# Expert steps of two units, new fill tables, and pair 1's front inside pair 0's first block

## The chip, the cores and the metric

The kernel runs on one core of a Trainium2 chip. A core has five engines that run side by side: TensorE (PE; its weight loads are listed as PEld), VectorE (DVE), ScalarE (ACT), GpSimd (POOL) and SyncE (SP), which here only starts DMAs. Each engine works through its own instructions in program order, and they wait for one another on semaphores. The metric is the device time of one execution in microseconds; lower is better.

## The reference, cut to what matters

```python
h = tok_ref(x, ...)                       # 16 images -> 49 patch tokens + cls, width 192 (convolutions, wavelets)
h = concatenate([h, txt], axis=1)         # + 128 text tokens -> 178 tokens an image
h = h + attn_ref(layernorm(h), ...)       # 12 heads of 16, diagonal masked except token 0, softmax, projection
h = h + ffn_ref(layernorm(h), ...)        # what follows:
    logits = gamma * zscore(Q @ K.T * scale)     # z-score of each row, then softmax, 12 heads
    x = layernorm(src + attn @ Wo.T + bo)
    gate_scores = softmax(x @ Wg.T + bg)         # 4 experts, the best 2 of each token are kept
    h = relu(x @ W1[e] + b1[e]); y = h @ W2[e] + b2[e]   # 192 -> 768 -> 192, all 4 experts
    ff = sum(y * combine); out = layernorm(x + ff)
```

All data is float32. Queries and keys are cut into three bfloat16 parts; the first expert matrix and its input are cut into a high and a low part.

## The kernel before, in words

**Stages.** The token stage (convolutions) takes the first part of the program. Then the 16 images are treated as 8 *pairs*. A pair goes through three blocks: block 0 is the first attention (`s = 0`), block 1 the second one (`s = 1`), and the third is the experts (MoE). They are pipelined over *rounds*: a round runs block 0 of pair `a`, block 1 of pair `b = a - 1`, the front of block 0 (turn-in, query, key, value) of pair `nxt = a + 1`, and the experts of pair `m = a - 2`. Engines run `pe_round`, `act_round`, `dve_round`, `sp_round` and `pool_round`, each with this same order, called by `rounds` (L1496). Round 0 has only `a = 0, nxt = 1`; round 1 has `a = 1, b = 0, nxt = 2`; rounds 2 to 6 are complete; round 7 has `a = 7, b = 6, m = 5`; round 8 has `b = 7, m = 6`; the last has `m = 7` alone.

**An attention block.** The input is normalised on DVE (`xn`), turned by PE (`pe_turn_in`), copied by ACT, projected to query and key (`pe_query`, `pe_key`), evacuated by ACT, split by DVE (`dve_split`), stored to DRAM and loaded back stacked (`stack` on SP). A *max pass* computes all logits once so that DVE can take the row maxima (`pe_max_pass`, `dve_max_pass`, 6 steps of two heads); the maxima are turned, copied and put as three more rows under the queries by DMA (`stack_max`); an *exp pass* computes the logits again with the maximum in them, ACT exponentiates, and PE multiplies by the values (`pe_values`). `pe_out` and `dve_out` normalise, project and add. Block 1 also has a *deviation* part (`pe_deviation`, `act_deviation`) that ends in the factor of the z-score, with which DVE scales the query before its split (`query` in `dve_front1`). After block 1 of pair `b`, DVE makes `x2`, PE turns it (L964), ACT and DVE make `x2T_hi` and `x2T_lo`, and PE computes the gate (L977).

**The experts as filling.** The experts of a pair are 24 *units* of 128 hidden channels. A unit has a *first* part F(u), five matmuls over 370 columns (L644) into PSUM bank `4 + u % 2`, the ReLU on ACT (L679) into `hid[u % 2]`, and a *second* part S(u), three float32 products of 192 columns, shown as six matmuls (L666). After every sixth unit DVE adds the expert's result to `acc` (L694, `expert`), which waits for that unit's second part. The class `Moe` cuts this into half steps: 0 is F(0), 1 is nothing, 2 is F(1), 3 is S(0), 4 is F(2), 5 is S(1), and so on to 48 (turning `comb`, S(23)) and 49 (`bias`, L654). At each named point of a round, `moe.point(name)` issues the number of half steps that the table says (`FILL`, in round 7 `FILL_A7`, in round 8 `FILL_B7`), on PE, ACT and DVE alike; `moe.rest()` issues what is left, in `pe_round` after the next pair's key and ahead of the turning of `x2`. The key places in `pe_round` are: "start"; turn-in of block 1; "norm"; query; "query"; key; "key"; value; the deviation part with "kc", "g", "u"; "ss"; max pass 0; ("split", 0); ("rows", 0); exp pass 0; max pass 1; ("split", 1); out of block 0 with ("turn", 0), ("back", 0); ("rows", 1); exp pass 1; out of block 1 with ("turn", 1), ("back", 1); the next turn-in; "next norm"; query; "next query"; key; rest. `("rows", 1)` stands under `if a is not None`, so that round 8 skips it.

**The beginning.** Before round 0 pair 0's front is computed, then `act_weights` and `dve_weights` cut the expert weights, which lie in four raw pieces of 1536 columns in `probs`, `qst1` and `kst1`; `dve_weights` ends with setting part of `kst1` to one (L1426), since that buffer held raw weights until then. Round 0 runs block 0 of pair 0 and then the front of pair 1, whose text is loaded into `h0` only once pair 0's residual has been added (`res_ready`).

## Time and profile before

| | |
|---|---|
| median of 3 runs | 1287.3 us (1286.83 to 1294.15) |
| the profiled execution | 1291.78 us, its span 1290.0 us |
| PE busy | 1095.4 us, 85% |
| DVE, ACT busy | 682.1 us, 399.7 us |
| mean granted TensorE clock | 0.884 |

By the stages of the profile: the token stage and pair 0's front last until 199.4 us, round 0 until 268.0, round 1 until 396.6, rounds 2 to 6 take 119.5 to 119.9 us each and end at 994.9, round 7 ends at 1117.2, round 8 at 1227.4, and the last round's experts run until 1279.0. The boundaries are the first turn-in of a round, or its gate's end.

How to read it: a busy time of PE is modelled from the start of each matmul, and the records of two neighbours overlap, so the distance from start to start is the better length. Idle time is shown in brackets with what ended it; "issue" means that no semaphore in the profile explains it.

### The profile page before, as it was taken

Reading aid. Unit: us, or ns where it says so; the run is one execution under the profiler, and the core shown is the slowest. Engines: PE = TensorE matmul, PEld = TensorE weight load, DVE = VectorE, ACT = ScalarE, POOL = GpSimd, SP = SyncE. Lnnn points to the kernel's source line nnn. Section 1 sums busy time; section 2 is a strip of 40 time slices with the busy share of each in tenths; the row PEclk is TensorE's granted clock in tenths of the full one; section 3 lists DMA queues with packets and bytes.
Section 4 is the critical chain, followed back from the end, with each engine's and each line's share of the span. In section 5 each row is a group of like instructions: output and inputs, shape, how many; then the busy total and the mean of one; then the engine's idle time right before and its main releaser. Section 6 shows DMA issues by size and latency. Waiting matters only on the chain.

```text
span 1290.0 us, 18666 instructions
## 1 busy us (share of the span) xinstructions
PE 1095.4 (85%) x7404; PEld 802.2 (62%) x7404; DVE 682.1 (53%) x1874; ACT 399.7 (31%) x905; POOL 54.1 (4%) x89
## 2 busy tenths in 40 slices
PE   7898645587779999999999999999999999985896
PEld 4343323354448668857776786678578667773795
DVE  1467685345454466654763674655557652632332
ACT  1222221212232433334323434333343234221321
POOL 6011100000000000000000000000000000000000
PEclk9898855755779989989998999899999989895988
DMA  8000051053005202320422043014204220022000
GB/s 296 0 1 0 16 152 26 7 97 61 11 7 119 49 8 56 78 43 9 84 51 44 8 105 66 13 34 100 44 8 82 51 43 2 1 64 29 1 10 8
DMA packets 38478, 60.74 MB, mean 47 GB/s; under 512 B 5060, under 2 KB 30264, under 8 KB 38072
## 3 DMA queue, kind: packets, MB, share of 16 engines
q1 hardware_dynamic: 36112, 56.84, 20.5%
q10 hardware_dynamic: 2280, 2.72, 0.7%
q8 instruction: 58, 0.95, 0.3%
q14 instruction: 28, 0.23, 0.1%
HBM read 42.76 MB, written 16.34 MB: 46 GB/s over the span
## 4 chain that ended last, share of the span: by engine, by line
PE 63%; DVE 13%; ACT 4%; issue 3%; DMA 3%; SPq 1%; POOL 0%; DVEq 0%; ACTq 0%; POOLq 0%
PE PS L666 14%; PE PS L644 11%; PE PS L755 7%; DVE mx L1271 6%; PE PS L849 5%; PE PS L763 5%; PE PS L790 5%; PE PS L796 3%; PE PS L805 2%; PE PS L858 2%; DMA qst<-mrows 1%; PE PS L887 1%; PE PS L977 1%; ACT probs L1031 1%; SPq L1471 1%
## 5 line engine op out<-in xcount | busy, mean ns | idle before, releaser
L666 PE MATMUL PS<-w,hid 128*128 128x192 f32 x1152 | 232.1, 339 | 3.0 <-DVE acc L694 1.8
L679 ACT ACTIVATE hid<-PS,b 128x370 f32<-128x370 f32 x192 | 109.1, 569 | 331.6 <-PE PS L644 329.8
L666 PEld LDWEIGHTS PS<-w,hid 128*128 128x128 f32 x1152 | 199.0, 197 | 12.8 <-issue 4.7
L1271 DVE TENSOR_REDUCE mx<-PS 128x2 f32<-128x356 f32 x288 | 129.8, 522 | 131.6 <-PE PS L790 103.5
L1031 ACT ACTIVATE probs<-PS 128x356 f32<-128x356 f32 x288 | 112.9, 484 | 35.6 <-PE PS L790 20.6
L790 PE MATMUL PS<-kst,qst 96*128 96x178 bf16 x384 | 71.5, 284 | 31.7 <-DMA kst<-scr_k 13.6
L644 PE MATMUL PS<-x2T_hi,w_hi 128*128 128x370 f32 x192 | 91.7, 478 | 0.0
L755 PE MATMUL PS<-xT,w_at 96*96 96x370 f32 x192 | 76.0, 546 | 8.9 <-ACT q L998 5.2
L805 PE MATMUL PS<-masks,ident_bf 128*128 128x256 bf16 (+1 forms) x288 | 79.9, 278 | 0.0
L790 PE MATMUL PS<-qst,kst 99*128 99x178 bf16 x384 | 58.0, 254 | 21.7 <-DMA qst<-mrows 17.5
L849 PE MATMUL PS<-probs,va 128*17 128x178 f32 x1536 | 70.8, 327 | 6.4 <-ACT probs L1031 6.4
L790 PEld LDWEIGHTS PS<-kst,qst 96*128 96x128 bf16 x384 | 27.2, 106 | 66.0 <-DVE mx L1271 30.7
L1292 DVE RECIPROCAL rs<-PS 128x36 f32<-128x36 f32 x16 | 6.1, 383 | 114.4 <-PE PS L858 114.4
L644 PE MATMUL PS<-x2T_hi,w_lo 128*128 128x370 f32 x192 | 66.2, 345 | 0.0
L644 PE MATMUL PS<-x2T_lo,w_hi 128*128 128x370 f32 x192 | 66.1, 344 | 0.0
L644 PE MATMUL PS<-x2T_hi,w_rest 128*128 128x370 f32 x192 | 66.1, 344 | 0.0
L644 PE MATMUL PS<-x2T_lo,w_rest 128*128 128x370 f32 x192 | 65.6, 342 | 0.0
L755 PEld LDWEIGHTS PS<-xT,w_at 96*96 96x96 f32 x192 | 33.4, 182 | 41.9 <-ACT q L998 8.9
L790 PEld LDWEIGHTS PS<-qst,kst 99*128 99x128 bf16 x384 | 28.7, 101 | 46.9 <-issue 30.8
L849 PEld LDWEIGHTS PS<-probs,va 128*17 128x17 f32 x1536 | 41.0, 99 | 24.4 <-ACT probs L1031 9.3
L694 DVE SCALAR_TENSOR_TENSOR acc<-PS,comb,acc 128x192 f32<-128x192 f32 x72 | 25.5, 410 | 54.3 <-PE PS L666 54.2
L377 DVE SCALAR_TENSOR_TENSOR dwo<-pad_l,chan,dwo 96x441 f32<-96x441 f32 x48 | 38.0, 793 | 27.9 <-ACT cw L301 26.4
(222 smaller groups left out, 1724.4 us busy)
## 6 DMA issues: line engine op xcount, KB each, us to landing
qst<-scr_q SPq DMA_DIRECT2D x96, 144.0 KB, 4.8
scr_q<-qs SPq DMA_DIRECT2D x16, 432.0 KB, 3.3
scr_k<-ks SPq DMA_DIRECT2D x16, 432.0 KB, 4.7
kst<-scr_k SPq DMA_DIRECT2D x16, 432.0 KB, 5.0
kst<-scr_k SPq DMA_DIRECT2D x16, 288.0 KB, 5.9
cols<-in_x_cols SPq DMA_DIRECT2D x6, 392.0 KB, 8.2
w<-in_w SPq DMA_DIRECT2D x1, 2304.0 KB, 25.2
kst<-scr_k SPq DMA_DIRECT2D x16, 144.0 KB, 6.3
```

What stands on the lines that cost most here:

```text
L377: ch.link(nc.vector.scalar_tensor_tensor(out=out, in0=image_rows(PAD_OF[r][:, 0, :], tap_offset(t), n), scalar=col(C_DW + 18 * r + t), in1 ...
L644: ins = nc.tensor.matmul(PS[:, 4 + u % 2, 0:XN], w[:, f], x[:, plane, 0:XN], start=(k == 0), stop=(k == 4))
L666: ins = nc.tensor.matmul(tile_psum((6, 7), i), hid[u % 2][:, 128 * i:128 * i + 128], w2[:, u, :], start=(j == 0 and i != 1), stop=(j == FT ...
L679: nc.scalar.activation(hid[u % 2][:, 0:XN], PS[:, 4 + u % 2, 0:XN], ACT.Relu, bias=b1[:, u:u + 1]).then_inc(S["h_ready"], 1)
L755: ins = nc.tensor.matmul(PS[0:HC, FRONT[s][m], 0:XN], w_at[:, w, k, HC * m:HC * m + HC], x[:, k, 0:XN], start=(k == 0), stop=(k == 1))
L763: ins = nc.tensor.matmul(tile_psum(banks, i), tile_cols(x, k, i), w_at[:, w, k, :], start=(k == 0), stop=(k == 1))
L790: ins = nc.tensor.matmul(PS[:, bank, T * b:T * b + T], still[0:rows_, h, TP * b:TP * b + NTXT], move[0:rows_, h, TP * b:TP * b + T], start ...
L796: ins = nc.tensor.matmul(PS[64 * b:64 * b + 64, 2, T * g:T * g + T], still[0:rows_, 2 * u + g, TP * b + NTXT:TP * b + TP], move[0:rows_, 2 ...
L805: ins = nc.tensor.matmul(own, ident_bf[:], m.rearrange("p (b j) -> p b j", b=2), start=False, stop=True, skip_group_check=True)
L849: ins = nc.tensor.matmul(PS[32 * q:32 * q + VW, 3, T * b:T * b + T], va[s][:, 2 * i + b, h, :], pr, start=(i == 0), stop=(i == 1), skip_gr ...
L1031: nc.scalar.activation(probs[:, u % PROB_UNITS, bank, :], PS[:, bank, 0:T2], ACT.Exp)\
L1271: nc.vector.tensor_reduce(out, PS[:, g, 0:T2].rearrange("p (b j) -> p b j", b=2), AX.X, ALU.max)\
```

## The change

It has four parts.

1. **Half steps of two units.** `MOE_STEPS` goes from 50 to 26. Step (d, even) is F(2d) and F(2d+1), step (d, odd) is S(2d) and S(2d+1). All fill tables are rewritten for it. Step (12, even) only turns `comb`. DVE's expert sums follow the odd steps of d = 2, 5, 8 and 11. `("rows", 1)` is now issued in every round.
2. **The bias behind the turning.** `pe_round` issues all steps but the last, turns `x2`, and only then issues the bias step. DVE's and ACT's order stays: all steps, then `x2T`.
3. **Pair 1's front inside pair 0's block.** Round 0 is replaced by `pe_first`, `act_first`, `dve_first` and `sp_first`. Pair 1's input lies in `h1_fin` instead of `h0`, its text is loaded at the start (semaphore `txt_early`), and its front uses PSUM banks 4 and 5.
4. **Raw weights in other pieces.** 1536, 1536, 2304 and 768 columns, in `probs` and `qst1` only, so that `kst1` is free and is set to one at the start of the token stage; the chain in `dve_weights` is one shorter.

```diff
-MOE_STEPS = 2 * UNITS + 2
+DUOS = UNITS // 2
+MOE_STEPS = 2 * DUOS + 2
 FILL = {
-    "start": 4, "norm": 1, "query": 4, "key": 3, "value": 0, "kc": 2, "g": 2, "u": 1, "ss": 2,
-    ("max", 0): (0, 0, 0, 0, 0, 0), ("split", 0): 2, ("rows", 0): 4, ("exp", 0): (0, 0, 0, 0, 0, 0), ("out", 0): 0,
-    ("max", 1): (0, 0, 0, 0, 0, 0), ("split", 1): 2, ("turn", 0): 2, ("back", 0): 1, ("rows", 1): 1,
-    ("exp", 1): (1, 0, 1, 1, 0, 2), ("out", 1): 0, ("turn", 1): 2, ("back", 1): 1, "next turn": 0, "next norm": 3,
-    "next query": 2,
+    "start": 2, "norm": 1, "query": 2, "key": 2, "value": 0, "kc": 1, "g": 1, "u": 1, "ss": 1,
+    ("max", 0): (0, 0, 0, 0, 0, 0), ("split", 0): 1, ("rows", 0): 2, ("exp", 0): (0, 0, 0, 0, 0, 0), ("out", 0): 0,
+    ("max", 1): (0, 0, 0, 0, 0, 0), ("split", 1): 1, ("turn", 0): 1, ("back", 0): 1, ("rows", 1): 0,
+    ("exp", 1): (0, 1, 0, 1, 0, 1), ("out", 1): 0, ("turn", 1): 1, ("back", 1): 0, "next turn": 0, "next norm": 2,
+    "next query": 1,
 }
 FILL_A7 = {
-    "start": 4, "norm": 4, "query": 4, "key": 0, "value": 0, "kc": 1, "g": 2, "u": 1, "ss": 2,
-    ("max", 0): (0, 1, 0, 0, 0, 0), ("split", 0): 2, ("rows", 0): 4, ("exp", 0): (1, 0, 0, 0, 0, 0), ("out", 0): 0,
-    ("max", 1): (0, 0, 1, 0, 0, 0), ("split", 1): 2, ("turn", 0): 2, ("back", 0): 1, ("rows", 1): 0,
-    ("exp", 1): (1, 2, 0, 0, 0, 1), ("out", 1): 1, ("turn", 1): 2, ("back", 1): 0, "next turn": 0, "next norm": 4,
+    "start": 2, "norm": 2, "query": 2, "key": 0, "value": 0, "kc": 1, "g": 1, "u": 0, "ss": 1,
+    ("max", 0): (0, 0, 0, 0, 0, 0), ("split", 0): 1, ("rows", 0): 2, ("exp", 0): (0, 0, 0, 0, 0, 0), ("out", 0): 0,
+    ("max", 1): (0, 0, 0, 0, 0, 0), ("split", 1): 1, ("turn", 0): 1, ("back", 0): 1, ("rows", 1): 0,
+    ("exp", 1): (0, 1, 0, 0, 0, 1), ("out", 1): 0, ("turn", 1): 1, ("back", 1): 0, "next turn": 0, "next norm": 0,
...
 FILL_B7 = {
-    "start": 4, "norm": 1, "query": 3, "key": 4, "value": 0, "kc": 2, "g": 0, "u": 2, "ss": 14,
-    ("max", 0): (0, 0, 0, 1, 1, 0), ("split", 0): 0, ("rows", 0): 0, ("exp", 0): (0, 0, 0, 0, 0, 0), ("out", 0): 1,
-    ("max", 1): (0, 0, 0, 0, 0, 0), ("split", 1): 1, ("turn", 0): 1, ("back", 0): 2, ("rows", 1): 4,
-    ("exp", 1): (1, 2, 0, 0, 0, 2), ("out", 1): 1, ("turn", 1): 2, ("back", 1): 0, "next turn": 0, "next norm": 3,
+    "start": 0, "norm": 0, "query": 2, "key": 1, "value": 0, "kc": 0, "g": 0, "u": 0, "ss": 10,
+    ("max", 0): (0, 0, 0, 0, 0, 0), ("split", 0): 0, ("rows", 0): 0, ("exp", 0): (0, 0, 0, 0, 0, 0), ("out", 0): 0,
+    ("max", 1): (0, 0, 0, 0, 0, 0), ("split", 1): 1, ("turn", 0): 0, ("back", 0): 0, ("rows", 1): 3,
+    ("exp", 1): (0, 1, 0, 0, 0, 1), ("out", 1): 0, ("turn", 1): 1, ("back", 1): 0, "next turn": 0, "next norm": 0,
...
@@ the token stage's DVE block
-                    nc.vector.memset(kst[0][SROWS:128, :, :], 1.0)
                     for s in range(2):
+                        nc.vector.memset(kst[s][SROWS:128, :, :], 1.0)
@@ buffers
+        W1_PARTS = ((0, 0, 1536, flat_probs[:, 0:1536]), (0, 1536, 3072, flat_probs[:, 1536:3072]),
+                    (1, 0, 2304, flat_qst[:, 0:2304]), (1, 2304, 3072, flat_probs[:, 3072:3840]))
+        def front(s, r):
+            return (2, 3) if s else (4, 5) if isinstance(r, int) and r == 1 else (0, 1)
+        def h_in(r):
+            return h1_fin if isinstance(r, int) and r == 1 else h0
@@ class MoePe
+            def step(self, d, odd):
                 pe, m = self.eng, self.m
+                if odd and d == DUOS:
                     self.bias()
                 elif odd:
+                    for u in range(2 * d, 2 * d + 2):
+                        self.second(u)
+                elif d == DUOS:
                     pe.wait_ge(S["comb_ready"], at(m, 1, 1))
...
+                else:
+                    for u in range(2 * d, 2 * d + 2):
+                        self.first(u)
@@ class MoeDve
+                elif odd and (2 * d + 2) % FT == 0:
+                    self.expert((2 * d + 2) // FT - 1)
@@ pe_round, and the like for ("rows", 1) in act_round and dve_round
             if a is not None:
                 pe_out(pe, 0, a, moe)
-                moe.point(("rows", 1))
+            moe.point(("rows", 1))
+            if a is not None:
                 pe.wait_ge(S["pr_read", 0], at(a, 1, 1))
...
-            moe.rest()
+            moe.steps(MOE_STEPS - 1 - moe.done)
             if b is not None:
                 pe.wait_ge(S["x2_ready"], at(b, 1, 1))
...
                 ins.then_inc(S["x2T_psum"], 1)
+            moe.rest()
@@ in place of round 0
+        def pe_first(pe):
+            pe_turn_in(pe, 0, 0)
+            pe_query(pe, 0, 0)
+            pe_key(pe, 0, 0)
+            pe_value(pe, 0, 0)
+            pe_turn_in(pe, 0, 1)
+            pe_query(pe, 0, 1)
+            none = NoMoe()
+            pe.wait_ge(S["v_ready", 0], 1)
+            pe_max_pass(pe, 0, 0, none)
+            pe_max_rows(pe, 0, 0)
+            pe_key(pe, 0, 1)
+            pe_exp_pass(pe, 0, 0, none)
+            pe.wait_ge(S["e_done", 0], 3 * HH)
+            pe_out(pe, 0, 0, none)
+            pe.wait_ge(S["pr_read", 0], 1)
+            pe_value(pe, 0, 1)
+        def act_first(act):
+            act_turn_in(act, 0, 0)
+            act_query(act, 0, 0)
+            act_key(act, 0, 0, None)
+            act_weights(act)
+            act_turn_in(act, 0, 1)
+            act.wait_ge(S["q_split", 0], 1)
+            act_query(act, 0, 1)
+            act.wait_ge(S["w_split"], 1)
+            act_max_rows(act, 0, 0)
+            act.wait_ge(S["k_split", 0], 1)
+            act_key(act, 0, 1, None)
+            none = NoMoe()
+            act_exp_pass(act, 0, 0, none)
+            act_out(act, 0, 0, none)
+        def dve_first(dve):
+            none = NoMoe()
+            tok_norm(dve, 0, 1)
+            splits = dve_front0(dve, 0)
+            tok_norm(dve, 1, PAIRS)
+            splits(None)
+            dve_value(dve, 0, 0)
+            splits = dve_front0(dve, 1)
+            dve_weights(dve)
+            dve_max_pass(dve, 0, 0, none)
+            dve.wait_ge(S["q_stored", 0], 16)
+            dve.wait_ge(S["k_stored", 0], 16)
+            splits(None)
+            dve_out(dve, 0, 0, none)
+            dve_norm1(dve, 0)()
+            dve_value(dve, 0, 1)
+        def sp_first(sp):
+            stack(sp, 0, 0, "q")
+            stack(sp, 0, 0, "k")
+            stack_max(sp, 0, 0)
+            stack_store(sp, 0, 1, "q")
+            stack_store(sp, 0, 1, "k")
+            sp.wait_ge(S["pv_psum", 0], 3)
+            stack_load(sp, 0, 1, "q")
+            stack_load(sp, 0, 1, "k")
-            one_round(eng, 0, None, 1, None, FILL)
@@ gpsimd
                 nc.gpsimd.memset(h0[:, 2, :], 0.0)
+                nc.gpsimd.memset(h1_fin[:, 2, :], 0.0)
...
                 pool.wait_ge(S["tok_ready"], 2)
+                image(pool, 1)
                 rounds(pool, pool_round)
```

## Rows read from the trace of the kernel before

**Rows 1.** The page's parts 1 and 2: engines, and TensorE's granted clock in 40 slices.
```profile
PE 1095.4 (85%) x7404; PEld 802.2 (62%) x7404; DVE 682.1 (53%) x1874; ACT 399.7 (31%) x905; POOL 54.1 (4%) x89
...
PEclk9898855755779989989998999899999989895988
```

**Rows 2.** Busy by stage: window, its length, busy of PE, PEld, DVE, ACT, POOL; clock.
```profile
199.40:249.50 50.10, 29.03 (x259) 17.85 (x260) 21.80 (x71) 10.43 (x27) 1.35 (x3) 0.67 0.02 5
...
516.50:636.30 119.80, 113.43 (x878) 87.50 (x876) 71.47 (x212) 44.45 (x105) 2.52 (x4) 0.97 0.25 50
...
1117.20:1227.40 110.20, 84.94 (x569) 68.85 (x566) 41.85 (x114) 30.24 (x66) 1.33 (x2) 0.84 0.14 28
```

**Rows 3.** Timeline of DVE, pair 0's front to round 0: start, us, what.
```profile
162.46 0.88 DVE L1123 BATCH_NORM_STATS2 stat<-h 128x6 f32<-128x192 f32 x3 [1.10 <-POOL h L1402]
...
166.02 0.96 DVE L1135 TENSOR_SCALAR xn<-h,mv,lsc 128x192 f32<-128x192 f32 x3
...
186.38 0.71 DVE L1156 TENSOR_TENSOR va<-PS,rows 50x192 f32<-50x192 f32 x2
...
196.07 3.90 DVE L1426 MEMSET kst<- 32x4608 bf16 x1 [1.02 <-issue]
...
244.62 0.17 DVE L151 SCALAR_TENSOR_TENSOR lsc<-lsc 128x3 f32<-128x3 f32 x1
```

**Rows 4.** Timeline of PE in the same stretch, to round 1's first turn-in.
```profile
199.42 0.46 PE L790 MATMUL PS<-kst,qst 96*128 96x178 bf16 x2 [13.56 <-DMA kst<-scr_k]
...
212.25 0.80 PE L823 MATMUL PS<-ident,mpart 128*36 128x128 f32 x3 [2.71 <-DVE mpart L1280]
...
217.54 0.46 PE L790 MATMUL PS<-qst,kst 99*128 99x178 bf16 x2 [4.50 <-DMA qst<-mrows]
...
251.85 5.00 PE L755 MATMUL PS<-xT,w_at 96*96 96x370 f32 x8 [0.88 <-ACT xT L991]
...
268.01 1.49 PE L747 MATMUL PS<-ident,xn 128*96 128x128 f32 x6
```

**Rows 5.** The page's part 5: a unit's first matmul and its second one.
```profile
L644 PE MATMUL PS<-x2T_hi,w_hi 128*128 128x370 f32 x192 | 91.7, 478 | 0.0
...
L644 PE MATMUL PS<-x2T_hi,w_lo 128*128 128x370 f32 x192 | 66.2, 345 | 0.0
```

**Rows 6.** Timeline of PE in the last round: two units in a row.
```profile
1236.17 0.47 PE L644 MATMUL PS<-x2T_hi,w_hi 128*128 128x370 f32 x1
...
1237.15 1.14 PE L666 MATMUL PS<-w,hid 128*128 128x192 f32 x6
1237.99 0.47 PE L644 MATMUL PS<-x2T_hi,w_hi 128*128 128x370 f32 x1
```

**Rows 7.** Who PE waited for in round 7: total us, times, longest.
```profile
PE PS L763 <- ACT oT L1048: 0.9, 1, 0.9
PE PS L790 <- DVE h L1304: 0.9, 1, 0.9
```

**Rows 8.** Timeline of PE at the end of round 2: next turn-in, gate.
```profile
491.56 0.82 PE L747 MATMUL PS<-ident,xn 128*96 128x128 f32 x6
...
512.34 0.24 PE L977 MATMUL PS<-gate_a,x2T_hi 128*128 128x8 f32 x1
```

**Rows 9.** Timeline of DVE there: splits, last expert sum, x2T_lo.
```profile
500.77 0.52 DVE L1142 CAST qs<-q 96x712 bf16<-96x712 f32 x1
...
507.13 1.07 DVE L694 SCALAR_TENSOR_TENSOR acc<-PS,comb,acc 128x192 f32<-128x192 f32 x3 [0.42 <-PE PS L666]
...
511.23 0.96 DVE L1389 TENSOR_TENSOR x2T_lo<-PS,x2T_hi 128x768 fp32r<-128x768 f32 x1 [0.81 <-ACT x2T_hi L1114]
```

**Rows 10.** Timeline of DVE in round 8, before block 1's max pass.
```profile
1152.74 1.07 DVE L694 SCALAR_TENSOR_TENSOR acc<-PS,comb,acc 128x192 f32<-128x192 f32 x3 [12.64 <-PE PS L666]
1153.84 0.96 DVE L1257 SCALAR_TENSOR_TENSOR q<-q,chan,rem 96x712 f32<-96x712 f32 x1
```

**Rows 11.** Timeline of PE there: what its max pass waited.
```profile
1170.02 0.75 PE L790 MATMUL PS<-kst,qst 96*128 96x178 bf16 x4 [13.03 <-issue]
```

**Rows 12.** Who PE waited for in the last round.
```profile
PE PS L666 <- DVE acc L694: 1.4, 3, 0.5
PE PS L654 <- DVE acc L694: 1.2, 1, 1.2
```

More of the change, by code:

```diff
@@ L111 @@
+    ("exp", 1): (0, 1, 0, 0, 0, 1), ("out", 1): 0, ("turn", 1): 1, ("back", 1): 0, "next turn": 0, "next norm": 0,
+    "next query": 0,
 }
@@ L670, in build, with step @@
         class MoeAct(Moe):
-            def step(self, u, odd):
+            def step(self, d, odd):
                 act, m = self.eng, self.m
-                if not odd and u < UNITS:
+                if odd:
+                    return
+                if d == DUOS:
+                    act.wait_ge(S["ct_psum"], at(m, 1, 1))
+                    nc.scalar.copy(combT[:, 0:XN], PS[0:E, 4, 0:XN]).then_inc(S["ct_ready"], 1)
+                    return
+                for u in range(2 * d, 2 * d + 2):
                     act.wait_ge(S["h_psum"], at(m, UNITS, u + 1))
@@ L727, in build, with steps @@
         class NoMoe:
+            done = 0
             def rest(self):
+                pass
+            def steps(self, n):
                 pass
@@ L995, in act_query @@
             for h in range(2):
[L996 removed]
+                for src, c in zip(by_token(front(s, r)[h]), (slice(0, NTXT), slice(NTXT, T))):
                     if s == 0:
@@ L1009, in act_key @@
             for h in range(2):
-                for src, c in zip(by_token(FRONT[s][h]), (slice(0, NTXT), slice(NTXT, T))):
+                for src, c in zip(by_token(front(s, r)[h]), (slice(0, NTXT), slice(NTXT, T))):
                     if s == 0:
@@ L1406, in act_weights @@
         def act_weights(act):
-            act.wait_ge(S["raw_in"], 16 * 2 * WCH)
-            for n in range(2 * WCH):
-                nc.scalar.copy(w1_part(n), raw[n]).then_inc(S["w_cast"], 1)
+            act.wait_ge(S["raw_in"], 16 * len(W1_PARTS))
+            for rest, lo, hi, raw in W1_PARTS:
+                nc.scalar.copy((w1_rest if rest else w1_hi)[:, lo:hi], raw).then_inc(S["w_cast"], 1)
         def dve_weights(dve):
```

137 lines of the change are left out of this document (58 added, 79 removed).

## The prediction, made before the changed kernel was run

> **What bounds the kernel now.** I read the page first: PE is busy for 85% of the span, twice as long as ACT and more, and its granted clock falls from 0.9 to 0.5 and 0.7 in the slices of rounds 0 and 1, again near the end [rows 1]. The busy times by stage then show three regimes [rows 2]. Round 0 has no expert work: PE is busy 29.0 of 50.1 us, at a clock of 0.67, and latencies between engines set its length. In a complete round PE is busy 113.4 of 119.8 us at 0.97; there are five of these, so there the time is PE's own work plus the few places where no filling covers a wait. Round 8 has 84.9 of 110.2 us busy at 0.84. So a change of order pays where PE has nothing to do (rounds 0, 1, 8), and in rounds 2 to 6 it can only move waits, each counted five times.
>
> **Pair 1's front.** Before, round 1 starts at 268.01, after pair 1's turn-in, query, key and value. In the new order it needs only `xn` of block 1. Step by step. DVE finishes pair 0's value at 187.1, and then does pair 1's normalisation, which took 162.46 to 166.98 for pair 0, 4.5 us; it lost the 3.9 us memset behind the weights, so the weights end at 199.97 + 4.5 - 3.9 - 1.0 (the gap ahead of the memset) = 199.6 [rows 3]. The memset itself is moved to the head of the token stage, where DVE then waits for loads; I price it at 0, and at 3.9 us if that wait were not there. PE gets `xn` at 191.7, needs 1.5 for the turn, 0.9 for ACT's copy and 5.0 for the query at the low clock, and is done at 199.1; the max pass began at 199.42 on the DMA of the keys and still does [rows 4]. The four extra text DMAs are issued on SP before it waits for the query split, 1.3 us of an idle queue: 0. POOL's extra memset and two copies are also in idle time: 0. Behind the turn of the maxima (ends 213.05) PE now does pair 1's key, 5.0 us as the query at the low clock, to 218.1, where the exp pass began at 217.54 [rows 4]; ACT evacuates that key (1.3 us) ahead of its first exponential, 219.5 in place of 218.25. Cost 1.3 us; the bounds are 0 (high clock) and 3. Pair 0's residual sum's root ends at 244.79 [rows 3], now 246.1; `xn` takes 0.96 (the row at 166.02), so round 1's turn-in starts at 247.1. Pair 1's value, 4 us of PE, ends before that. Gain 268.0 - 247.1 = **20.9 us**. What is late next is the same chain as before, block 0's end into block 1's front; the splits of pair 1 lie in the exp pass, where DVE is idle.
>
> **The order of two units.** A unit takes 1237.99 - 1236.17 = 1.82 us from start to start [rows 6]: F is 0.85 and S 0.97. The first matmul of a unit is shown as 478 ns, the others as 345 [rows 5], and in the new order every other F follows an F instead of an S. A plain reading gives 96 times 133 ns = 12.8 us of gain. I take 0: the 12 instructions of 192 columns and 370 columns, read from start to start, fill the 1.82 us if each S instruction takes 0.162 us and each F one 0.17, and the six S then reach 0.14 us into the record of the next F. The Trainium skill ("TensorE: Matmul & The Clock Gate", Part 1) states that the distance of back-to-back matmuls is set by their columns and the clock, with about 2.5 ns on top; by that rule the sum stays as it is. The means of the records, taken at their word, remain a rival below. S(2d) must wait for the ReLU of F(2d), 0.57 us under F(2d+1), 0.85 us: 0.
>
> **Rounds 2 to 6.** The same 24 F and 24 S are issued, so only covers change; I went slot by slot with F = 0.85 and S = 0.97. ("rows", 1) goes from one F to nothing, and PE waits for DVE to read the projection; ("back", 1) goes from one F to nothing, and PE waits for ACT's copy. Both already stand so in `FILL_A7`, where the waits are 0.9 us each [rows 7]: +0.85 each. "norm" and "u" had an F against latencies of about 1.05 and 1.15 and get two units' worth: -0.2 and -0.3. Split 0 gets 0.1 more: -0.1. Exp pass 1 gets one S more in its idle spots: -0.4 (0 to -1.0). The end of the round is the largest. Before, from turn-in to gate it is 512.34 - 491.56 = 20.8 us with 4 F and 6 S in it [rows 8]; the new table has 2 F and 4 S there, so 17.15 us if nothing waits. But the last expert sum now comes ahead of DVE's two splits instead of behind them [rows 9], and PE has only the turning of `comb`, of `x2`, the bias and the value after the key. DVE: S(23) ends 8.7 us after the turn-in, sum until 10.5, query split until 13.5, key split until 16.5 (500.77 to 506.7 is 6.0 us for both), bias 0.95, `x2T_lo` 0.96: the gate starts at 18.5, +1.4 (bounds +0.3 and +4.6, the whole F and S that followed the key). The 1.16 us wait ahead of the bias, which disappears by the new place of the bias, is inside that figure. DVE's second expert sum now comes ahead of block 1's query split, 1.1 us later into a DMA that landed about 1.5 us early: +0.1 (0 to 1.1). Sum per round: 1.7 - 0.6 - 0.4 + 1.4 + 0.1 = +2.2, five times **+11**, bounds 0 and +27.
>
> **Round 7.** "u" has no step any more, +0.9; three steps that stood inside passes go to the rest, +1.3 by half their length; the end has the bias wait covered, -0.9: **+1.3**, bounds -1 and +4.
>
> **Round 8.** This is where the new table looks best and does least. PE waited 13.0 us for block 1's stacked query [rows 11], and the query was late because DVE stood 12.64 us in the expert sum that "ss" contains, with the query scaling right behind it [rows 10]. The new "ss" has 10 double steps, and its second sum needs S(11), that is 8 F and 10 S after the deviation product, 16.5 us, where it was 5 F and 5 S and a wait of 1.1, 10.2 us: +6.3. The front before it has 4 F and 2 S instead of 8 F and 7 S, 8.2 us less work, of which waits of 3 to 6 us appear: -2 to -5, and PE is at its low clock for part of it. So the max pass starts 1 to 4 us later, though PE idles there again. The newly reached ("rows", 1) fills the 4.4 us wait for the maxima but can run over it by 3 at the low clock, exp pass 1 is shorter by as much, and the end wins 2.4 with less rest work ahead of `x2`'s turning and no bias wait. Together **-1**, bounds -5 and +4.
>
> **Last round.** Waits for the sums of 1.4 us are covered by a second F: -1.2; the bias wait of 1.2 loses what the turning of `comb` covers: -0.3 [rows 12]. **-1.5**.
>
> **Sum.** -20.9 + 11 + 1.3 - 1 - 1.5 = -11 us. Against the profiled execution's 1291.8 us this is 1280.8; the median of the runs is 4.5 us lower, 1287.3, and -11 makes **1276 us**, 0.9% less. About 1%, 12.9 us, is what a measurement here tells from no change, so 1274.4 and 1300.2 are the borders.
>
> **Rivals.** (1) *Moved covers cost nothing.* Small waits of 0.9 us could be taken back where another engine catches up; for it: PE never waits over 1.2 us in a complete round. Against it: the same two slots do show 0.9 in round 7. Rounds 2 to 6 at 0 give -22, 1265. (2) *The longer record is real*: -11 - 12.8 = -24, 1263. Against it: the sum of starts above. (3) *Half the overlap*: ACT has pair 1's key and query ahead of the exponentials and DVE pair 1's norm ahead of the weights; if PE's and DVE's 5 us each fall on the chain, 10 of the 20.9 us go, 1286. For it: both are within 0.3 us of the DMA that hides them. (4) *Slower than before, by the end of the round*: after the last key nothing covers DVE's chain expert sum, two splits, bias, `x2T_lo`. Should the sum start late, the gate comes 4.6 us later instead of 1.4, and rounds 2 to 6 cost 27: with the rest, +5, 1292. It decides from 2.2 us more a round on; only with round 8 at its bad bound as well would it pass 1300. (5) *The change doesn't do what it says* holds for round 8 alone, and is in the sum.
>
> **Chances.** The forecast 0.53, ±6 about 1276, of which a third lies below 1274.4; rival 1 0.17, rival 2 0.06, rival 3 0.12, rival 4 0.12. Faster by over 1%: 0.18 + 0.17 + 0.06 and a little = 0.42. Slower by over 1%: 0.08, from the end of rival 4. Within 1%: 0.50. The range takes in rivals 1 and 3 and most of 4: 1263 to 1291.
>
> **What would show it.** Round 1's first turn-in at 247, not 268 us. Complete rounds of about 122 us in place of 119.8, with new waits of 0.8 us at L763 and L790, a wait of 2 us or more ahead of L977, and none ahead of L654. The means of L644's first matmul lower, but a unit pair still 3.64 us from start to start. In round 8 DVE's longest wait for L666 near 16 us and PE's wait for the max pass above 13. The forecast is wrong if complete rounds stay at 119.8 or grow by over 4 us, or if the exp pass of pair 0 starts after 221.

## The result, and the profile after

| | before | changed |
|---|---|---|
| median of 17 runs each, on one chip | 1289.79 us (1283.86 to 1297.93) | 1300.54 us (1288.67 to 1313.86) |
| ratio to before | | **1.0066, 95% [1.0043, 1.0090]** |
| the profiled execution | 1291.78 us | 1313.86 us, span 1312.1 us |
| mean granted TensorE clock | 0.884 | 0.868 |

The changed kernel is a little slower, within 1%. The forecast was 1276.0 us, within 1% too, but on the other side, and 1300.5 lies outside its range. The profiled execution of the changed kernel is the longest and slowest of its 17 runs, so its stages overstate the usual loss; experiment 6, profiled at 1295.12 us with the same code up to round 7, is set beside it below.

The page, parts 1 and 2, answers to [rows 1]:

```profile
PE 1126.7 (86%) x7404; PEld 831.0 (63%) x7404; DVE 680.4 (52%) x1874; ACT 399.1 (30%) x905; POOL 56.3 (4%) x90
...
PEclk9898867656789898989898999799988999886998
```

PE has the same 7404 instructions and is busy 31.3 us longer. DVE and ACT are not. Its mean granted clock is lower (0.868, before 0.884), and single records below are longer where the clock is low (a gate product 0.35 us, before 0.24); the second half of the last row has eight digits under 9 where it had seven. The busy times by stage, columns as in [rows 2]: pair 0's block (the max pass to round 1's turn-in), one complete round, round 8.

```profile
201.00:248.70 47.70, 37.82 (x286) 22.99 (x284) 25.83 (x64) 12.30 (x35) 0.66 (x1) 0.79 0.35 65
...
634.60:760.90 126.30, 116.66 (x877) 91.83 (x876) 71.78 (x211) 44.42 (x105) 2.48 (x4) 0.93 0.24 47
1133.90:1252.50 118.60, 94.10 (x584) 75.18 (x585) 44.26 (x127) 31.59 (x69) 1.42 (x2) 0.82 0.13 26
```

**Pair 1's front** took the path that was forecast. PE's timeline, against [rows 4]:

```profile
197.11 1.51 PE L762 MATMUL PS<-ident,xn 128*96 128x128 f32 x6 [6.49 <-DVE xn L1193]
...
204.94 0.31 PE L805 MATMUL PS<-kst,qst 96*128 96x178 bf16 x2 [0.52 <-DMA kst<-scr_k]
...
221.00 0.33 PE L805 MATMUL PS<-qst,kst 99*128 99x178 bf16 x2
...
222.98 0.33 PE L805 MATMUL PS<-qst,kst 99*128 99x178 bf16 x2 [0.85 <-ACT probs L1070]
...
248.67 1.52 PE L762 MATMUL PS<-ident,xn 128*96 128x128 f32 x6 [1.14 <-DVE xn L1193]
```

Pair 1's turn and query stand in what was one 13.56 us wait for the keys' DMA; 6.49 us of it are left ahead of the turn and 0.52 ahead of the max pass. The exp pass starts at 221.00, right behind pair 1's key, so nothing is left of the 4.50 us wait for the maxima; the 0.85 us stand one step later, for ACT's exponentials. In this execution the whole beginning is 5.3 us late (pair 0's turn-in at 172.39, 167.1 before). Round 1 starts at 248.67 in place of 268.01; counted from pair 0's turn-in that is 76.3 us in place of 100.9, a gain of 24.6 where the forecast has 20.9. Part of the rest is clock: behind pair 1's turn and query the max pass runs at the high level, and DVE's row maxima, which follow it, take 7.93 us in place of 9.97.

**By stages**, measured from gate to gate (the gate is the product on `gate_a`, L977 before, L994 after):

| | before | after | difference | forecast |
|---|---|---|---|---|
| to round 1's gate | 390.9 | 373.3 | -17.6 | -20.9 |
| rounds 2 to 6 | 599.8 | 635.3 | **+35.5** | +11 |
| round 7 | 119.4 | 122.8 | +3.4 | +1.3 |
| round 8 | 114.8 | 119.3 | +4.5 | -1 |
| gate of round 8 to the end | 65.0 | 61.4 | -3.7 | -1.5 |

The sum is +22.1, the difference of the two spans (1312.1 - 1290.0). The five complete rounds take 122.9, 129.3, 126.3, 129.8 and 127.0 us. Experiment 6, with the same code in the first three rows, has -22.4, +28.7 and +3.4 there.

**The end of a complete round.** PE's timeline, against [rows 8]; L661 is the bias, L994 the gate, L673 the second parts of the first two units, and the last row the next round's turn-in:

```profile
747.12 1.21 PE L661 MATMUL PS<-b,hid 4*128 4x192 f32 x6 [0.82 <-ACT hid L686]
...
751.89 0.35 PE L994 MATMUL PS<-gate_a,x2T_hi 128*128 128x8 f32 x1 [1.15 <-DVE x2T_lo L1450]
...
757.67 3.42 PE L673 MATMUL PS<-w,hid 128*128 128x192 f32 x12
760.92 0.82 PE L762 MATMUL PS<-ident,xn 128*96 128x128 f32 x6
```

From the next pair's turn-in (733.85) to the gate it is 18.0 us; 18.5 was forecast. But from the gate to block 1's turn-in it is 9.0 us, where two first and two second parts at 0.85 and 0.97 and the gate's 1.3 make 5.0. One gate instruction is 0.35 us long, 0.24 in [rows 8]; twelve matmuls of the second parts are 3.42 us, 2.18 elsewhere. Windows of 10 us about this place, after (first three) and before (last three), columns as above; the middle one of each begins 2 us ahead of the gate:

```profile
739.90:749.90 10.00, 9.18 (x48) 6.92 (x48) 9.62 (x19) 3.98 (x10) 0.00 (x0) 1.00 0.17 44
749.90:759.90 10.00, 8.85 (x33) 8.38 (x32) 5.47 (x21) 1.35 (x3) 0.00 (x0) 0.51 0.82 133
759.90:769.90 10.00, 10.00 (x54) 8.64 (x54) 6.60 (x27) 4.06 (x9) 0.00 (x0) 0.98 0.45 90
```
```profile
859.20:869.20 10.00, 8.84 (x51) 7.39 (x50) 8.26 (x16) 2.77 (x7) 0.00 (x0) 1.00 0.39 86
869.20:879.20 10.00, 9.88 (x58) 8.28 (x58) 6.82 (x25) 3.46 (x6) 0.00 (x0) 1.00 0.86 148
879.20:889.20 10.00, 10.00 (x54) 8.57 (x53) 8.54 (x28) 3.93 (x11) 0.00 (x0) 1.00 0.26 62
```

The column to read is the granted clock behind ACT's and POOL's. PE falls to its low level (0.5, that is 1.2 in place of 2.4 GHz) for about ten microseconds, from 750.1 to 760.3: these cover the wait ahead of the gate, the gate and the start of the next round, with 33 instructions in the window where there were 58. PE's busy share hardly says so: what 8.85 lacks is the wait of 1.15 us. This was the theory to test: **two bare waits of 0.8 and 1.15 us cost 2 us as waits, and up to 4 us more as clock.** Two limits of it stand in the same rows. The fall at 750.1 comes 3 us behind the first wait (which ends at 747.12) and ahead of the second (750.74 to 751.89), so here the second one did not start it. And the same end does not always cost the same: in the profile all five ends have about 10 us at the low level and take 8.7 to 9.0 us from gate to turn-in (the stretch starts 1.8 to 2.6 us ahead of the gate in each), but in experiments 2, 3 and 6, where the end has much the same waits, six of the fifteen ends have only 3.4 us, which start behind the gate, and take 6.6 to 6.7.

### The profile page after: what moved, and what is told of

Same layout as the page of the kernel before. It is cut to its first block, busy times and chain, and to the rows that moved or that the text cites. A ratio compares the mean times of both kernels' runs of the same rounds, so it can differ in the third digit from the quotient of the medians.

```text
span 1312.1 us, 18666 instructions
## 1 busy us (share of the span) xinstructions
PE 1126.7 (86%) x7404; PEld 831.0 (63%) x7404; DVE 680.4 (52%) x1874; ACT 399.1 (30%) x905; POOL 56.3 (4%) x90
## 4 chain that ended last, share of the span: by engine, by line
PE 58%; DVE 18%; ACT 4%; issue 4%; DMA 2%; SPq 1%; POOL 0%; DVEq 0%; POOLq 0%; ACTq 0%
PE PS L651 12%; PE PS L673 12%; DVE mx L1332 6%; PE PS L770 5%; PE PS L864 5%; PE PS L805 5%; PE PS L778 4%; PE PS L811 3%; PE PS L873 2%; PE PS L820 2%; PE PS L994 1%; PE PS L902 1%; ACT probs L1070 1%; DMA qst<-mrows 1%; PE PS L914 1%
## 5 line engine op out<-in xcount | busy, mean ns | idle before, releaser
L673 PE MATMUL PS<-w,hid 128*128 128x192 f32 x1152 | 222.0, 346 | 0.1
L673 PEld LDWEIGHTS PS<-w,hid 128*128 128x128 f32 x1152 | 202.3, 203 | 10.6 <-issue 1.3
L805 PE MATMUL PS<-kst,qst 96*128 96x178 bf16 x384 | 69.4, 276 | 24.5 <-issue 18.3
L770 PE MATMUL PS<-xT,w_at 96*96 96x370 f32 x192 | 80.3, 571 | 7.9 <-ACT xT L1030 4.4
L651 PE MATMUL PS<-x2T_hi,w_hi 128*128 128x370 f32 x192 | 82.0, 427 | 0.6 <-ACT mrows L1061 0.6
L820 PE MATMUL PS<-masks,ident_bf 128*128 128x256 bf16 (+1 forms) x288 | 76.9, 268 | 0.0
L651 PE MATMUL PS<-x2T_lo,w_hi 128*128 128x370 f32 x192 | 68.9, 359 | 0.0
L651 PE MATMUL PS<-x2T_hi,w_rest 128*128 128x370 f32 x192 | 68.8, 358 | 0.0
L651 PE MATMUL PS<-x2T_lo,w_rest 128*128 128x370 f32 x192 | 68.3, 356 | 0.0
L864 PEld LDWEIGHTS PS<-probs,va 128*17 128x17 f32 x1536 | 40.7, 99 | 23.6 <-ACT probs L1070 7.8
## 6 DMA issues: line engine op xcount, KB each, us to landing
cols<-in_x_cols SPq DMA_DIRECT2D x6, 392.0 KB, 14.6
```

Source lines behind the costliest of these rows:

```text
L651: ins = nc.tensor.matmul(PS[:, 4 + u % 2, 0:XN], w[:, f], x[:, plane, 0:XN], start=(k == 0), stop=(k == 4))
L673: ins = nc.tensor.matmul(tile_psum((6, 7), i), hid[u % 2][:, 128 * i:128 * i + 128], w2[:, u, :], start=(j == 0 and i != 1), stop=(j == FT ...
L770: ins = nc.tensor.matmul(PS[0:HC, banks[m], 0:XN], w_at[:, w, k, HC * m:HC * m + HC], x[:, k, 0:XN], start=(k == 0), stop=(k == 1))
L805: ins = nc.tensor.matmul(PS[:, bank, T * b:T * b + T], still[0:rows_, h, TP * b:TP * b + NTXT], move[0:rows_, h, TP * b:TP * b + T], start ...
L820: ins = nc.tensor.matmul(own, ident_bf[:], m.rearrange("p (b j) -> p b j", b=2), start=False, stop=True, skip_group_check=True)
L864: ins = nc.tensor.matmul(PS[32 * q:32 * q + VW, 3, T * b:T * b + T], va[s][:, 2 * i + b, h, :], pr, start=(i == 0), stop=(i == 1), skip_gr ...
```

## The experiments

Each was timed against the kernel before on the same chip. Ratios are to the kernel before, with 95% intervals; the changed kernel's is 1.0066.

**1. Parts 3 and 4 alone.** Before, with `pe_first` and its like, the early text and the raw pieces; tables, steps and bias untouched.

> The kernel before with part 3 (pair 1's front inside pair 0's first block) and part 4 (the raw weights in other pieces) alone; one-unit half steps, the three fill tables and the place of the bias as before. Theory A: the overlap is worth what the changed kernel's trace shows, round 1's first turn-in 19.3 us earlier (268.0 to 248.7) and its gate 17.6 us earlier, and nothing after it moves, so the time is 17 to 20 us below the kernel before (ratio about 0.985 to 0.987), complete rounds stay at 119.5 us. Rival B: the overlap is given back in rounds 1 and 2 (TensorE at its low clock where the start was compressed), so it is worth 10 us or less (ratio above 0.992).

Measured: 1270.03 us, ratio **0.9841 [0.9807, 0.9875]**, -20.8 us. Complete rounds 119.5. The overlap is worth what was forecast in all. In the trace round 1 gives 1.7 us back (124.6 from its turn-in to its gate, 122.9 before), nothing after it does.

**2. Parts 1 and 2 alone.** Before, with the two-unit steps, the new tables and the bias behind the turning.

> The kernel before with parts 1 and 2 (two-unit steps, their fill tables, the bias behind the turning) alone; the start as before. Theory A: the whole loss is in these two parts; complete rounds take 126 to 129 us in place of 119.5, and with round 8 and the last the time is 25 to 35 us above the kernel before (ratio 1.02 to 1.027). Forecast's price: 2.2 us a round, +10 in all (ratio 1.008). Rival B: the changed kernel's long rounds come from its other memory layout or from the start being compressed; then this kernel's rounds stay near 120 and the ratio near 1.00.

Measured: 1324.99 us, ratio **1.0262 [1.0225, 1.0299]**, +34. Rounds 2 to 6 take 624.4 us (before 599.8), round 8 120.6. Experiments 1 and 2 add up to 1.010: the change is a gain of 21 us and a loss of 30 to 34.

**3. The bias ahead of the turning again.**

```diff
-            moe.steps(MOE_STEPS - 1 - moe.done)
+            moe.rest()
...
-            moe.rest()
```

> The changed kernel with the bias step put back ahead of the turning of x2 (part 2 undone); everything else as changed. Theory A (the loss is in the tables, which leave nothing for TensorE after the last key): the place of the bias matters little, within 1 us a round either way, ratio to the changed kernel 0.995 to 1.005. Rival C (the bias behind the turning is itself the loss, because the turning now waits bare for x2 and the clock falls): rounds come down by 3 us or more each, ratio to the kernel before about 0.992.

Measured: 1302.04 us, ratio 1.0094 [1.0059, 1.0130]. No effect that can be told from the changed kernel; the loss is in part 1, the two-unit steps with their tables, which no run takes apart.

**4. The last second parts behind the last key.**

```diff
-    ("exp", 1): (0, 1, 0, 1, 0, 1), ("out", 1): 0, ("turn", 1): 1, ("back", 1): 0, "next turn": 0, "next norm": 2,
+    ("exp", 1): (0, 1, 0, 1, 0, 1), ("out", 1): 0, ("turn", 1): 1, ("back", 1): 0, "next turn": 0, "next norm": 1,
```

> The changed kernel with one number changed in the table of the complete rounds: next norm 2 becomes 1, so that the second parts of the last two units (1.9 us of TensorE) come after the last key in place of ahead of it, and DVE's last expert sum behind its splits. Theory A (TensorE runs at its low clock from about 5 us before the gate until 10 us behind it because nothing fills the end of the round): the gate to the next turn-in... is shorter, from 9.0 us back towards 5.5, complete rounds 2 to 4 us shorter, the time 10 to 20 us below the changed kernel. Forecast's view (only the wait counts): the wait ahead of the gate falls from 1.1 us, at most 1 us a round, 5 us in all. Rival D: the loss lies in the passes (maxima turn to maxima turn 28 to 29.5 us in place of 26.7), then nothing changes.

Measured: 1325.26 us, ratio **1.0270 [1.0236, 1.0305]**: 25 us *slower* than the changed kernel, where 10 to 20 us faster was expected. The trace shows what the expectation had left out; PE, then DVE:

```profile
753.23 2.28 PE L661 MATMUL PS<-b,hid 4*128 4x192 f32 x6 [3.43 <-DVE acc L704]
```
```profile
751.30 0.90 DVE L1203 TENSOR_TENSOR ks<-rem,ks 96x712 bf16<-96x712 f32 x1
752.12 1.06 DVE L704 SCALAR_TENSOR_TENSOR acc<-PS,comb,acc 128x192 f32<-128x192 f32 x3
```

With the step after the key, DVE's last expert sum falls behind both splits, and PE waits 3.43 us for it, although 1.9 us of work more stand in front. The end got emptier, not fuller: turn-in to gate 22.0 us in place of 18.0, and at the low level until 17 us after the wait began. One number in the table moves a step on three engines; this one had to be costed on DVE.

**5. The end filled with work for nobody.** `fill_pe(5)` ahead of the bias and `fill_pe(6)` ahead of the gate, wherever a round has both experts and a next pair. That is rounds 2 to 6 (55 such matmuls in the trace), not 7 as the expectation has it.

```diff
+        def fill_pe(n):
+            for _ in range(n):
+                nc.tensor.matmul(PS[:, 5, 0:XN], w1_hi[:, 0:128], w1_hi[:, 0:XN], start=True, stop=True)
```

> The changed kernel with extra TensorE work whose result nobody reads, in rounds 2 to 7: five matmuls of 370 columns on constant weights ahead of the bias step, and six ahead of the gate. Theory A: TensorE's granted clock falls to its low level (10 us of 0.50 in the profiled execution of the changed kernel) at the end of a round because what is left there is two bare waits (0.8 and 1.1 us) and small instructions; with 1.9 us of work more a round the low stretch ahead of the gate goes, the time from the gate to the next round's turn-in falls from 9.0 to about 5.3 us, and the kernel is 10 to 18 us FASTER than the changed one although it does more. Forecast's view (only the waits cost): 1.9 us of extra work into 2.0 us of wait, no change, or slower by up to 1 us a round, +6. Rival E (the fall has its cause earlier in the round, in the passes): the low stretch stays, +0 to +10.

Measured: 1288.06 us, ratio **0.9981 [0.9957, 1.0005]**, 12.5 us faster than the changed kernel with 1.9 us more work a round. PE's timeline at the same place:

```profile
734.44 1.10 PE L920 MATMUL PS<-w_hi 128*128 128x370 f32 x5
...
738.57 1.32 PE L920 MATMUL PS<-w_hi 128*128 128x370 f32 x6
740.29 0.24 PE L1003 MATMUL PS<-gate_a,x2T_hi 128*128 128x8 f32 x1 [0.40 <-DVE x2T_lo L1459]
...
743.43 2.18 PE L673 MATMUL PS<-w,hid 128*128 128x192 f32 x12
745.44 0.82 PE L762 MATMUL PS<-ident,xn 128*96 128x128 f32 x6
```
```profile
738.20:748.20 10.00, 9.60 (x63) 9.02 (x62) 6.60 (x24) 2.83 (x6) 0.00 (x0) 1.00 0.74 135
```

Turn-in to gate stays at 18.0 (DVE sets it), the clock stays at 1.00, and gate to turn-in is 5.1 us: the 5.0 reckoned above. From the second of these ends on every round has it; the first has 3.4 us at the low level and takes 6.6. This experiment decides between the two theories: had only waits counted, work could not have made it faster. It fills both waits at once, so which of the two has to be covered was not separated.

**6. Round 8's table spread.**

```diff
-    "start": 0, "norm": 0, "query": 2, "key": 1, "value": 0, "kc": 0, "g": 0, "u": 0, "ss": 10,
+    "start": 2, "norm": 1, "query": 1, "key": 2, "value": 0, "kc": 1, "g": 0, "u": 1, "ss": 5,
```

> The changed kernel with round 8's table spread over the front as before the change, in two-unit steps: start 2, norm 1, query 1, key 2, kc 1, u 1, ss 5 in place of query 2, key 1, ss 10 (13 steps ahead of the max pass in both). Theory F: in round 8 the turn-in to the maxima's turn took 76.1 us after and 63.4 before, because ten steps after the deviation hold DVE in an expert sum with the query scaling behind it, while the front's waits stand empty; spread, that stretch comes back to 64 to 67 us less what start takes ahead of the turn-in, and gate to gate falls from 119.3 to 113 to 116, the kernel 3 to 6 us faster than the changed one. Rival G: the stretch is set by TensorE's total work at its low clock, not by the order; then it changes by 1 us or less.

Measured: 1292.73 us, ratio 1.0001 [0.9975, 1.0027], 8 us below the changed kernel; round 8 falls from 119.3 to 112.2 us. Both are a little more than was expected. Round 8 in the changed kernel, DVE and then PE, against [rows 10] and [rows 11]:

```profile
1170.58 1.07 DVE L704 SCALAR_TENSOR_TENSOR acc<-PS,comb,x_wide 128x192 f32<-128x192 f32 x3 [10.36 <-PE PS L673]
1181.77 1.07 DVE L704 SCALAR_TENSOR_TENSOR acc<-PS,comb,acc 128x192 f32<-128x192 f32 x3 [10.12 <-PE PS L673]
1182.87 0.95 DVE L1318 SCALAR_TENSOR_TENSOR q<-q,chan,rem 96x712 f32<-96x712 f32 x1
```
```profile
1198.35 0.75 PE L805 MATMUL PS<-kst,qst 96*128 96x178 bf16 x4 [15.00 <-issue]
```

Two expert sums now stand ahead of the query's scaling, each waiting 10 us, and the scaling comes 49.0 us after the turn-in, 36.6 before. In experiment 6 one sum waits, 12.01 us, and the scaling comes 35.6 us after the turn-in. PE's wait ahead of the max pass is no measure of the loss: 15.0 us in the changed kernel, 15.3 in experiment 6, 13.0 before.

**7. Experiment 1 with the bias behind the turning**, one-unit steps.

> The kernel before with pair 1's front overlapped (parts 3 and 4) and the bias step behind the turning of x2; one-unit steps and tables as before. Theory A: with S(23) still after the key the end of the round stays full, the turning of x2 (0.9 us) covers most of the bias's 1.16 us wait: 0 to 1 us a round gained, total 0 to -7 us against the kernel with parts 3 and 4 alone (1270.0). Rival C (the bias behind the turning is what brings the low clock): each round 2 us or more longer, 1282 or more.

Measured: 1264.09 us, ratio **0.9793 [0.9761, 0.9825]**, 6 us below experiment 1. The wait ahead of the bias is 0.5 us in place of 1.2, rounds 119.2. So part 2 is a small gain where the end of the round is full.

**8. Less at the end, one-unit steps.** Experiment 1 with `"next query": 4` in place of 2 in `FILL`.

> The kernel before with parts 3 and 4, and one number of the complete rounds' table changed: next query 2 becomes 4, so that the last F and two S go after the key in place of two F and three S; 1.8 us of TensorE's work stand ahead of the last key in place of behind it. One-unit steps all through. Theory A: turn-in to gate stays at 20.8 us, as DVE's splits and sum set it, but TensorE's wait ahead of the bias grows from 1.2 to about 3 us, and its clock falls there: gate to turn-in 6 to 8 us in place of 4.2, complete rounds 2 to 4 us longer, the kernel 10 to 20 us above the one with parts 3 and 4 alone (1270.0). Forecast's view (only waits cost, and this one is off DVE's path): no change, 0 to +1 us a round.

Measured: 1282.03 us, ratio **0.9926 [0.9900, 0.9951]**, +12 on experiment 1, rounds 122.0 to 123.1. The size was as expected, the place was not: from gate to turn-in it stays 4.2, with the clock high, in spite of a 2.28 us wait ahead of the bias. Only one of the five ends has a low stretch, 3.4 us from 1 us behind that wait on. Turn-in to gate grows by 1.0, because the key is later and with it DVE's key split (first row, a new wait of 1.54 us). Most of the rest is in the passes of the rounds that follow: in three of the five their low stretch is 10.2 us in place of 6.8 (table below).

```profile
727.70 0.53 DVE L1190 CAST ks<-k 96x712 bf16<-96x712 f32 x1 [1.54 <-ACT k L1042]
```
```profile
731.68 1.24 PE L656 MATMUL PS<-b,hid 4*128 4x192 f32 x6 [2.28 <-DVE acc L696]
```

**11. Experiment 8, its wait filled** with ten of the matmuls of experiment 5 ahead of the bias.

> The kernel with next query 4 (1.8 us of TensorE's work ahead of the last key in place of behind it, 1282.0 us) and ten matmuls of 370 columns on constant weights, 1.7 us, ahead of the bias, where it waits for DVE. Theory A: the 12 us that the moved work cost were TensorE's clock, not the order of the units, so the dummy work in its place brings complete rounds back from 122.9 to about 120 and the kernel to 1268 to 1273. Forecast's view and any rival by the order of the units or DVE's sums: the dummy work changes nothing or costs, 1282 or more.

Measured: 1278.07 us, ratio 0.9898 [0.9869, 0.9927]: 4 of the 12 us come back, not 9 to 14. Two rounds are at 121, one is at 122 and two stay at 123. The 1.0 us of the late key is order and not clock, 5 us of the 12; the expectation was wrong to call all of it clock. The other 3 or so go with the low level that is left (44.2 us, 37.4 in experiment 1) and were not separated.

**The low level, PE's waits and the length of rounds 2 to 6** (us, from round 1's gate to round 6's; the low time is 2 x (1 - clock), summed over windows of one microsecond under 0.97; the waits are all of PE's idle times over 0.15 us):

| kernel | low | waits | length |
|---|---|---|---|
| before; experiments 1 and 7 | 37.4 | 27.9; 27.9; 24.3 | 599.8; 599.0; 597.0 |
| experiments 11, 8 | 44.2, 51.0 | 24.6, 33.0 | 609.9, 613.3 |
| new tables: experiment 5 | 51.0 | 34.7 | 618.2 |
| experiments 3, 2, 6 | 71.4, 74.8, 84.2 | 43.8, 43.5, 42.0 | 624.3, 624.4, 628.5 |
| changed kernel, as profiled | 101.6 | 42.9 | 635.3 |
| experiment 4 | 104.7 | 51.5 | 648.7 |

The waits of the changed kernel are 15.0 us longer than before; the other 20.5 of the 35.5 us are no waits, and 64 us more lie at the low level. The same subtraction leaves 8.6, 9.0 and 14.6 us in experiments 3, 2 and 6, and 25.3 in experiment 4. That is 0.24 to 0.38 us for each microsecond more at the low level. In experiment 5 the 55 extra matmuls take 9.4 us by themselves, and only 2.2 are left. Up to 4 us in each of these remainders may be the order of two units (see there, below). Three executions of the very same rounds (experiments 2 and 6 and the changed kernel) have 75, 84 and 102 us at the low level, so this part varies from run to run, and with it the time: 9 to 20 us, most of it clock, on 14 to 16 us of waits.

**9. Round 8's query first on DVE**, on experiment 7.

```diff
                 query = dve_front1(dve, b, a, moe, last)
+                if a is None:
+                    query(a)
                 moe.point("ss")
...
-            if b is not None:
+            if b is not None and a is not None:
                 query(a)
```

> The kernel with pair 1's front overlapped and the bias behind the turning (one-unit steps, tables as before; 1264.1 us), and in round 8 DVE scales and splits block 1's query ahead of the ss steps in place of behind them; TensorE and ScalarE as they were. Theory F (in round 8 the query is late because DVE waits 12.64 us for the expert sum in the ss steps with the scaling behind it): the query's DMA starts 12 us earlier, TensorE's wait of 12.8 us ahead of the max pass falls under 2 us, gate to gate of round 8 falls from 114.0 to 102 to 105, the kernel at 1252 to 1256. Rival G (the ss work and the max pass then run at TensorE's low clock, or the expert sum comes late in turn): half of it, 1258.

Measured: 1252.62 us, ratio **0.9704 [0.9672, 0.9735]**, 11.5 us below experiment 7; round 8 takes 104.8 us. DVE, then PE:

```profile
1122.46 0.96 DVE L1309 SCALAR_TENSOR_TENSOR q<-q,chan,rem 96x712 f32<-96x712 f32 x1 [5.43 <-ACT rem L1097]
...
1129.72 1.07 DVE L696 SCALAR_TENSOR_TENSOR acc<-PS,comb,acc 128x192 f32<-128x192 f32 x3 [3.31 <-PE PS L668]
```
```profile
1138.45 0.75 PE L797 MATMUL PS<-kst,qst 96*128 96x178 bf16 x4 [4.49 <-issue]
```

The scaling no longer stands behind the sum's 12.64 us. PE's wait falls to 4.5, not under 2; the scaling now has a wait of its own, 5.43 us for ACT, which is likely the reason.

**10. Round 1 filled**, on experiment 9: at each point of round 1 where a later round has expert work, 5 to 25 of the dummy matmuls, 154 in the trace (the expectation counts 148).

> The same kernel as e9_query_first plus extra TensorE work in round 1, whose result nobody reads: 5 to 25 matmuls of 370 columns on constant weights at each point where a later round has expert work, 148 in all, 25 us at the high clock. Theory A (TensorE's low clock, not its work, makes round 1 long: 98 of the 125 us from its turn-in to its gate are at the low level, with waits of 1 us everywhere): with the waits filled the clock stays high, round 1 takes 118 to 121 us in place of 124.5 although TensorE does 25 us more; 4 to 7 us faster than the kernel without it. Forecast's view (work and waits only): 148 matmuls into some 25 us of waits, no gain, and 5 to 15 us slower where they run past a wait.

Measured: **1232.99 us, ratio 0.9555 [0.9526, 0.9584]**, 19.6 us below experiment 9, the fastest of all. Round 1, turn-in to turn-in: experiment 10, then experiment 1, which has no such work:

```profile
245.10:354.70 109.60, 100.82 (x772) 74.20 (x773) 61.90 (x177) 31.81 (x82) 2.02 (x4) 0.94 0.19 40
```
```profile
248.20:378.50 130.30, 98.75 (x619) 62.71 (x620) 63.27 (x177) 32.87 (x82) 2.01 (x4) 0.65 0.17 33
```

153 instructions more, PE busy for nearly the same time, the clock at 0.94 in place of 0.65, and 20.7 us less. The expectation had 4 to 7: the gain is that nearly all of PE's own work in the round runs at the high level.

**12. Pair 0's front and block filled too**, on experiment 10: 77 matmuls on the projection weights `w_at`, 4 to 20 a wait.

> The kernel e10_round1_filled (1233.0 us) plus extra TensorE work in the waits of pair 0's front and first block: 77 matmuls of 370 columns on the constant projection weights, 4 to 20 at each wait of 0.9 to 5.8 us. Theory A (the low clock of this stretch, 54 of the 80 us from the first turn-in to round 1's, comes from its waits): the clock rises and the 76 us between the first turn-in and round 1's become 66 to 72, the kernel 4 to 10 us faster. Rival H: this stretch hangs on ScalarE, VectorE and DMAs, and the matmuls at the low clock (0.31 us each, 24 us in all) run past the waits; then 0 to 8 us slower.

Measured: 1251.99 us, ratio 0.9698 [0.9660, 0.9735], 19 us *slower* than experiment 10. The dummy's group, then the two stretches:

```profile
L1016 PE MATMUL PS<-w_at 96*96 96x370 f32 x154 | 50.9, 484 | 0.0
```
```profile
165.00:200.00 35.00, 33.03 (x110) 18.78 (x111) 28.05 (x80) 9.22 (x13) 1.37 (x2) 0.91 0.50 128
200.00:262.00 62.00, 58.58 (x384) 34.62 (x381) 24.48 (x66) 14.88 (x37) 0.66 (x1) 0.94 0.25 44
```

The clock rose to 0.91 and 0.94, as theory A says, but the stretch took 93.3 us from the first turn-in to round 1's in place of 76.2. These weights are plain float32, and 77 products are 154 matmuls in the trace, where `w1_hi` makes one of each; the dose, 50.9 us where 24 were meant, ran past nearly every wait. Whether half of it would pay was not tried.

## Why the prediction was wrong, point by point

- **Pair 1's front**, -20.9: the path was right, and the total, -20.8 alone (experiment 1), is in part luck. Counted from pair 0's turn-in the gain at round 1's turn-in is 24.6, as the max pass runs at the high level, which the prediction had not counted; 1.7 are given back in round 1.
- **The order of two units**, 0: right that nothing is gained. (The 12 instructions of the prediction are six and five; its sum is right.) In the last round a pair of units is 3.75 and 3.73 us from start to start, and [rows 6] make 3.64:

```profile
1257.22 0.47 PE L651 MATMUL PS<-x2T_hi,w_hi 128*128 128x370 f32 x1
...
1260.97 0.47 PE L651 MATMUL PS<-x2T_hi,w_hi 128*128 128x370 f32 x1
...
1264.70 0.47 PE L651 MATMUL PS<-x2T_hi,w_hi 128*128 128x370 f32 x1
```

  The first matmul that follows another F has a shorter record, and nothing is gained by it; rival 2 falls. If anything it costs: between neighbours without a wait at the high level, the middle value of 46 units before is 1.83 us and that of 16 pairs after is 3.73, 0.06 us more a pair. That makes 6 us for the 96 pairs, an estimate, as the other pairs have different neighbours. By the Trainium skill ("TensorE: Matmul & The Clock Gate", Part 1) the distance of back-to-back matmuls goes by their columns and the clock, with about 2.5 ns on top. The trace agrees in that the order gains nothing. It does not in size: from one 370-column matmul to the next it has 0.17 us, where an estimate from the page's figures is 0.157, and the 0.06 us stand beside that.
- **Rounds 2 to 6**, +11, measured +35.5 in the profile and +24.5 to +28.7 in experiments 2, 3 and 6: **the step that failed.** The prediction says that "only covers change": each wait that the new table opens or closes is priced at its own length, for +2.2 us a round, and the clock of the round is left at 0.97. The waits were near enough. PE's waits, round 2's turn-in to round 7's, the changed kernel and then the one before:

```profile
PE PS L994 <- DVE x2T_lo L1450: 4.6, 5, 1.2
PE PS L805 <- DVE h L1365: 4.6, 5, 0.9
...
PE PS L778 <- ACT oT L1087: 4.4, 5, 0.9
PE PS L661 <- ACT hid L686: 4.1, 5, 0.8
```
```profile
PE PS L654 <- DVE acc L694: 5.8, 5, 1.2
```

  The two of 0.9 us came as named. At the end, where one of 2 us or more was forecast ahead of the gate and none ahead of the bias, there are 0.8 ahead of the bias and 0.4 to 1.2 ahead of the gate; the gate itself starts at 18.0, for 18.5. All waits together are up by 15.0 us. What was missing is that they are also paid in clock, most of the 9 to 20 us that the five rounds are longer by besides; experiment 5 takes most of it away and is 12.5 us faster. The 119.8 us round had been read as PE's own work plus a few waits, without asking what held the clock at 0.97.
- **Round 7**, +1.3, measured +3.4; it was not separated.
- **Round 8**, -1, measured +4.5. The place was right (DVE's sum blocks the query's scaling). Two sizes were not: from the deviation's product to the scaling it grew by 8.9 us (14.7 to 23.6), not 6.3, and DVE has two waits of 10 us there in place of one near 16; and the front, 8.2 us of work lighter, became no shorter but 3.4 longer from the turn-in, at the low clock. Experiment 6 takes both back with the old spread; experiment 9 moves only the scaling's place on DVE, on the old table, and round 8 is 9 us shorter.
- **Last round**, -1.5, measured -3.7: the three waits for the sums (1.4 us together in [rows 12]) are gone, that for the bias is 0.9. The rest is likely clock again, this time in favour: about the gate it was at the low level for 3.4 us, before for 10.2.
- **The rivals.** Rival 4 had the right place, the end of the round, and 27 us for the five rounds; its mechanism, a late sum, is what experiment 4 makes, not what the change does. Slower by over 1% had 0.08 and within 1% 0.50; the point forecast failed mainly by one term (round 8 adds 5.5 us to the miss), and the range by treating the clock in complete rounds as given.

## What to carry to other kernels

Where TensorE is the bound, short waits can cost their length once more, or twice, in clock (here 2 us of waits at the end of a round, and 1.6 to 4 us of clock). So cost a new wait by what runs behind it, and ask of a stretch at full clock what keeps it there. Where TensorE waits all along, matmuls that nobody reads can pay (here 154 of them saved 20 us), but size them by start to start in the trace, and stop at the length of the wait. Moving a filling step moves it on every engine: cost it on the engine whose order sets the end.
